# Graph convolutions of a four-layer GNN kernel: two scaled fp16 parts in place of three bf16 parts

## What is computed

```python
def _gcn_conv(x, src, dst, W, b):
    n = x.shape[0]
    h = x @ W
    deg = segment_sum(ones_like(dst), dst, num_segments=n) + 1.0
    dinv = lax.rsqrt(deg)
    norm = dinv[src] * dinv[dst]
    agg = segment_sum(h[src] * norm[:, None], dst, num_segments=n)
    return agg + h * (dinv * dinv)[:, None] + b
...
h = relu(_gcn_conv(x, src, dst, W1, b1))
h = relu(_gcn_conv(h, src, dst, W2, b2))
return _gcn_conv(h, src, dst, W3, b3)
```

## Time and profile before

| | us |
|---|---|
| median of 3 runs | 3300.55 (3297.96 to 3302.93) |
| the profiled execution, its own time | 3305.37 |
| its span | 3303.6 |
| TensorE matmul busy | 2807.4 (85%) |
| VectorE busy | 2368.9 (72%) |
| GpSimd busy | 1212.1 (37%) |
| ScalarE busy | 768.1 (23%) |

### The profile page before, as it was taken

The page is one execution under the profiler, slowest core; times in us unless marked ns, Lnnn a source line. Parts: engine busy times, 40 slices in busy tenths (PEclk is TensorE's granted clock), DMA queues, the critical chain, the costliest instruction groups (busy, mean ns, idle before and its releaser), DMA issues.

```text
span 3303.6 us, 73960 instructions
## 1 busy us (share of the span) xinstructions
PE 2807.4 (85%) x25677; PEld 2263.3 (69%) x25678; DVE 2368.9 (72%) x6272; ACT 768.1 (23%) x1414; POOL 1212.1 (37%) x1205
## 2 busy tenths in 40 slices
PE   3777777899999988998799999999598888988984
PEld 0211121699999987777699999998476777766763
DVE  6988777753333355325798888887699999999986
ACT  0123455520000005001111111111133333332321
POOL 0000000000000000000577777776177777777771
PEclk9999998889999997999899999999599999999896
DMA  0000000000000000000454444443233333433330
GB/s 29 0 0 0 0 0 0 2 2 2 2 2 2 1 1 5 1 1 10 99 132 117 119 115 117 120 119 77 57 104 103 105 105 106 107 104 101 105 97 22
DMA packets 108156, 180.81 MB, mean 55 GB/s; under 512 B 36346, under 2 KB 69900, under 8 KB 107867
## 3 DMA queue, kind: packets, MB, share of 16 engines
q0 software_dynamic: 47824, 89.19, 11.5%
q1 hardware_dynamic: 60043, 87.59, 9.3%
HBM read 171.88 MB, written 4.80 MB: 53 GB/s over the span
## 4 chain that ended last, share of the span: by engine, by line
POOL 32%; issue 10%; DVE 5%; PE 2%; DMA 1%; DVEq 0%; ACT 0%; POOLq 0%; ACTq 0%
POOL gate_rows L1327 20%; POOL msg_rows L956 13%; DVE pre_space L1030 2%; PE msg_sums L1152 1%; PE msg_sums L1167 0%; DMA first_rows<-pre_space 0%; DVE msg_rows L1054 0%; DVE pre_space L1450 0%; DMA msg_rows<-h_rows,all_src_i 0%; PE gate_sums L1581 0%; ACT msg_src_near L968 0%; DMA msg_src_row<-src_rows 0%; DVE pre_space L1122 0%; DVE msg_rows L1050 0%; DVE all_h L1518 0%
## 5 line engine op out<-in xcount | busy, mean ns | idle before, releaser
L1327 POOL DMA_INDIRECT gate_rows<-first_rows,all_src_i x637 | 655.1, 1028 | 198.3 <-issue 193.8
L956 POOL DMA_INDIRECT msg_rows<-h_rows,all_src_i x539 | 535.0, 993 | 164.1 <-issue 163.8
L943 POOL MEMSET pre_middle<- 125x1 f32 x1 | 0.1, 98 | 1590.8 <-POOLq L649 1590.8
L1152 PE MATMUL msg_sums<-pre_parts,pre_space 125*128 125x192 f16 x6125 | 530.7, 248 | 37.5 <-DVE pre_space L1030 37.3
L1152 PEld LDWEIGHTS msg_sums<-pre_parts,pre_space 125*128 125x128 f16 x6125 | 512.3, 99 | 44.3 <-DVE pre_space L1030 39.1
L579 PE MATMUL hop_sums<-dense_work,dense_counts 125*128 125x192 f16 x6250 | 520.7, 247 | 14.0 <-DVE dense_t L533 6.4
L579 PEld LDWEIGHTS hop_sums<-dense_work,dense_counts 125*128 125x128 f16 x6250 | 517.9, 98 | 16.6 <-DVE dense_t L533 6.9
L1556 PE MATMUL gate_sums<-pre_space,pre_parts 125*96 125x384 f16 x2450 | 459.7, 349 | 5.3 <-DVE pre_parts L1424 5.3
L422 PE MATMUL cnt_sums<-cnt_hot,cnt_near 128*128 x1000 | 347.9, 411 | 118.6 <-DVE cnt_hot L361 113.9
L1556 PEld LDWEIGHTS gate_sums<-pre_space,pre_parts 125*96 125x96 f16 x2450 | 315.3, 132 | 140.5 <-issue 30.8
L1030 DVE TENSOR_SCALAR pre_space<-msg_src_near,pre_node_no 125x640 f16<-125x640 f16 x1225 | 393.6, 395 | 11.6 <-ACT msg_src_near L968 11.3
(11 more groups left out here) (261 smaller groups left out, 3320.7 us busy)
## 6 DMA issues: line engine op xcount, KB each, us to landing
msg_edge<-edges SPq DMA_DIRECT2D x98, 384.0 KB
msg_src_row<-src_rows SPq DMA_DIRECT2D x49, 312.5 KB
gate_edge<-edges SPq DMA_DIRECT2D x98, 128.0 KB
gate_rows<-first_rows,all_src_i POOLq DMA_INDIRECT x637
gate_src_row<-on_src SPq DMA_DIRECT2D x49, 187.5 KB
msg_rows<-h_rows,all_src_i POOLq DMA_INDIRECT x539
gate_inputs<-on_edges SPq DMA_DIRECT2D x49, 48.0 KB, 1.9
first_rows<-pre_space SPq DMA_DIRECT2D x6, 375.0 KB
```

The source lines that it names most:

```text
L956: nc.gpsimd.indirect_dma_start(out=rows[:, r, k, :], out_offset=None, in_=table, in_offset=bass.IndirectOffsetOnAxis(ap=src_i[:, at:at + 1 ...
L1152: last = nc.tensor.matmul(got[group % 2][:, n, 0:2 * D], pick[:, c % 2, j, i * EP:(i + 1) * EP], parts[:, j, :], start=(j == 0), stop=(j = ...
L1327: nc.gpsimd.indirect_dma_start(out=rows[:, r, k, :], out_offset=None, in_=table, in_offset=bass.IndirectOffsetOnAxis(ap=src_i[:, at:at + 1 ...
```

## The change

The three bf16 parts become two fp16 parts of a scaled value. fp16 has a narrow range, so the kernel finds in each convolution the largest magnitude of `t` over all nodes, and scales by 30000 over that peak before it rounds.

- In the mixing phase L714 stays. The four splitting steps go; VectorE instead reduces each group to its largest and its smallest value per partition, two full passes over the group.
- After the last group VectorE joins the seven pairs to one value per partition, TensorE transposes that column into one row, VectorE reduces the row to one number, TensorE spreads the number over the partitions by a matmul with a row of ones, and VectorE makes the factor (`peak[:, 3:4]`) and its inverse (`peak[:, 2:3]`).
- Only then ScalarE writes the first parts of all seven groups (scaled by a factor that it reads per partition), and VectorE the second parts, each in one pass.
- The product phase begins with the first group's split. Its matmuls have 192 columns in place of 288; the drain reduces over two parts, and the addition of `t` becomes a multiply-add with the inverse factor.

```diff
-        parts = g["work"][0:NP, 0:NT * 3 * D].bitcast(BF16).rearrange("p (t d) -> p t d", t=NT)
+        parts = g["work"][0:NP, 0:NT * 2 * D].rearrange("p (t d) -> p t d", t=NT)
...
         @block.scalar
-            def split_parts(k, m0, n):
-
-                act.wait_ge(value, k + 1)
-                nc.scalar.activation(parts[:, m0:m0 + n, 0:D], t[:, m0:m0 + n, :], ACT.Copy).then_inc(first, 1)
-                act.wait_ge(rest, k + 1)
-                nc.scalar.activation(parts[:, m0:m0 + n, D:2 * D], h[:, m0:m0 + n, :], ACT.Copy).then_inc(second, 1)
...
-                    if q >= 1:
-                        split_parts(k - 1, *GROUPS[q - 1])
-                split_parts((c + 1) * ngr - 1, *GROUPS[-1])
+                act.wait_ge(scaled, c + 1)
+                for q, (m0, n) in enumerate(GROUPS):
+                    nc.scalar.activation(parts[:, m0:m0 + n, 0:D], t[:, m0:m0 + n, :], ACT.Copy,
+                                         scale=peak[:, 3:4]).then_inc(first, 1)
...
         @block.vector
+            link(nc.vector.memset(ones[:, :], 1.0))
...
                     nc.vector.tensor_tensor(t[:, m0:m0 + n, :], got, spread(dinv[:, m0:m0 + n], D),
                                             ALU.mult).then_inc(value, 1)
-                    dve.wait_ge(first, k + 1)
-                    nc.vector.tensor_tensor(h[:, m0:m0 + n, :], t[:, m0:m0 + n, :], parts[:, m0:m0 + n, 0:D],
-                                            ALU.subtract).then_inc(rest, 1)
-                    dve.wait_ge(second, k + 1)
-                    nc.vector.tensor_tensor(parts[:, m0:m0 + n, 2 * D:3 * D], h[:, m0:m0 + n, :],
-                                            parts[:, m0:m0 + n, D:2 * D], ALU.subtract).then_inc(split, 1)
+                    dve.wait_ge(value, k + 1)
+                    flat = t[:, m0:m0 + n, :].rearrange("p n d -> p (n d)")
+                    link(nc.vector.tensor_reduce(peaks[:, 0, q:q + 1], flat, AX, ALU.max))
+                    link(nc.vector.tensor_reduce(peaks[:, 1, q:q + 1], flat, AX, ALU.min))
+                link(nc.vector.tensor_reduce(peak[:, 0:1], peaks[:, 0, 0:ngr], AX, ALU.max))
+                link(nc.vector.tensor_reduce(peak[:, 1:2], peaks[:, 1, 0:ngr], AX, ALU.min))
+                nc.vector.scalar_tensor_tensor(out=peak[:, 2:3], in0=peak[:, 1:2], scalar=-1.0, in1=peak[:, 0:1],
+                                               op0=ALU.mult, op1=ALU.max).then_inc(peaked, 1)
+                dve.wait_ge(peak_turned, c + 1)
+                nc.vector.tensor_reduce(peak[0:1, 0:1], sums[0:1, 0, 0:NP], AX, ALU.max).then_inc(peaked, 1)
+                dve.wait_ge(peak_spread, c + 1)
+                link(nc.vector.tensor_scalar(peak[:, 2:3], sums[0:NP, 1, 0:1], TINY, 1.0 / TOP, ALU.max, ALU.mult))
+                nc.vector.reciprocal(peak[:, 3:4], peak[:, 2:3]).then_inc(scaled, 1)
+                dve.wait_ge(scaled, c + 1)
+                for q, (m0, n) in enumerate(GROUPS):
+                    dve.wait_ge(first, c * ngr + q + 1)
+                    nc.vector.scalar_tensor_tensor(out=parts[:, m0:m0 + n, D:2 * D], in0=t[:, m0:m0 + n, :],
+                                                   scalar=peak[:, 3:4], in1=parts[:, m0:m0 + n, 0:D], op0=ALU.mult,
+                                                   op1=ALU.subtract).then_inc(split, 1)
...
-                    three = sums[0:NP, 4 * (q % 2):4 * (q % 2) + n, 0:3 * D].rearrange("p n (a d) -> p n d a", a=3)
-                    nc.vector.reduce_sum(v, three, AX).then_inc(drained, 1)
+                    both = sums[0:NP, 4 * (q % 2):4 * (q % 2) + n, 0:2 * D].rearrange("p n (a d) -> p n d a", a=2)
+                    nc.vector.reduce_sum(v, both, AX).then_inc(drained, 1)
                     dve.wait_ge(drained, k + 1)
-                    link(nc.vector.tensor_tensor(v, v, t[:, m0:m0 + n, :], ALU.add))
+                    link(nc.vector.scalar_tensor_tensor(out=v, in0=v, scalar=peak[:, 2:3], in1=t[:, m0:m0 + n, :],
+                                                        op0=ALU.mult, op1=ALU.add))
...
         @block.tensor
                 mix(ngr - 1)
+                pe.wait_ge(peaked, 2 * c + 1)
+                nc.tensor.transpose(sums[0:1, 0, 0:NP], peak[:, 2:3], g["ident"][0:NP, 0:NP]).then_inc(peak_turned, 1)
+                pe.wait_ge(peaked, 2 * c + 2)
+                nc.tensor.matmul(sums[0:NP, 1, 0:1], ones[:, :], peak[0:1, 0:1], start=True, stop=True
+                                 ).then_inc(peak_spread, 1)
...
                     if q == 0:
-                        pe.wait_ge(value, (c + 1) * ngr)
+                        pe.wait_ge(scaled, c + 1)
...
-                            last = nc.tensor.matmul(sums[:, 4 * (q % 2) + i, 0:3 * D], counts[0:NP, at:at + 128],
+                            last = nc.tensor.matmul(sums[:, 4 * (q % 2) + i, 0:2 * D], counts[0:NP, at:at + 128],
                                                     parts[:, j, :], start=(j == 0), stop=(j == NT - 1))
```

More of the change, by code:

```diff
@@ L46 @@
 ROUND = 12582912.0
+TOP = 30000.0
+TINY = 1e-30
 WROW = 28
@@ L656, in convolutions @@
         b_sb = m.sb("b", [NP, 3, D], F32)
+        room = g["work"][0:NP, NT * 2 * D:NT * 3 * D].bitcast(F32)
+        peaks, peak, ones = room[:, 0:16].rearrange("p (i q) -> p i q", i=2), room[:, 16:20], room[0:1, 32:32 + NP]
         sums = m.ps("sums", [128, 8, BANK], F32)
@@ L661, in convolutions @@
         turned = m.sem("turned"); turned_out = m.sem("turned_out"); mixed = m.sem("mixed")
-        value = m.sem("value"); first = m.sem("first"); rest = m.sem("rest"); second = m.sem("second")
+        value = m.sem("value"); first = m.sem("first"); peaked = m.sem("peaked"); scaled = m.sem("scaled")
+        peak_turned = m.sem("peak_turned"); peak_spread = m.sem("peak_spread")
         split = m.sem("split"); summed = m.sem("summed"); drained = m.sem("drained"); passed = m.sem("passed")
```

## The result

The changed kernel takes 3225.74 us (median of four runs, 3217.22 to 3230.84), the kernel before 3299.74 (3297.96 to 3302.93): a ratio of 0.9772, 95% interval 0.9754 to 0.9789, 2.3% faster. Timed again (e1) the ratio is 0.9766 (0.9752 to 0.9780). The profiled execution took 3217.22 us with a span of 3215.5; its counterpart before 3305.37 with 3303.6. The spans differ by 88.1 us, more than the medians (74.0): the profiled execution of the changed kernel was the fastest of its four. That difference is taken apart first.

What follows compares the result with a forecast made beforehand. TensorE's matmuls bound the product phases, chains of handoffs the mixing phases. Terms 73.5 + 1.9 + 1.9 - 0.9 = 76.4 us, from 3300.55 to 3224.2 us, 2.3% faster; range 3215 to 3240.

Steps and rivals of the forecast that it cites:

- Full groups: Product phases: 100 matmuls at 82.5 ns in place of 122.5, each full group 4.0 us less.
- The rival of the weight loads: Product phases: weight loads no longer overlap and set a 98 ns spacing, 29 us less gain, 3253 us; chance 0.04.
- the step that I took from a load's length to the least spacing: Product matmuls: by the skill page, fewer columns stop paying at 106.7 ns, full groups falling only 1.6 us; not adopted.
- First groups: First group of each product phase: first drain 10.5 us after the first product in place of 14.50, 4.0 less.
- The slow stretch: Start of each product phase: half clock again lasts 4.05 us, in which 25 matmuls get done.
- The claim beside it: First group: the first 4 us' clock hardly matters, 0.2 us a convolution; at full clock splits bind, 10.3 us.
- Drain: Drains: reduction 958 ns, multiply-add 558; ends give 0.5 us each; convolution 3 still covered by 0.25 us.
- Mixing phases 2 and 3: Convolutions 2 and 3, first value to first product: 15.0 us in place of 16.89, 1.9 less each.
- Mixing phase 1: Convolution 1: half clock throughout, TensorE sets the pace at 2.45 us a group, products at 1309.7, a 0.9 us loss.
- the signs that the prediction had named: Trace signs, wrong if: spacing above 90 ns, half clock beyond 5 us, factor passes above 600 ns, another message-stage length.
- the costlier search: Search for the peak: dearer crossings cost 4.2 us, slower per-partition-factor passes some 13 us, 3237 us; chance 0.10.
- the half clock through the products: Product phases: TensorE stays at half clock after the new pause, 3363 us if for all 1875 matmuls; chance 0.03.

Runs made afterwards that it cites:

- e1: The changed kernel run again with no edit, for a second trace and a narrower ratio: 3229.99 us, ratio 0.9766.
- e3: Changed kernel with 288 columns again in every product matmul, the third part zero and its sums not read: 3301.4 us, ratio 0.9989.
- e11: Changed kernel with only the first part in products and sums, 96 columns a matmul, leaving out part of the computation: 3177.82 us, ratio 0.9640.
- e7: Changed kernel plus matmuls of no use on TensorE: 4 behind each mix, 30 in the search pause, 16 behind the spreading matmul: 3215.49 us, ratio 0.9754.
- e8: As e7, with the first group's four output tiles innermost in the loop, so each split feeds 16 matmuls, not 4: 3214.97 us, ratio 0.9755.
- e10: Changed kernel with e5's single reduction, e8's loop order, and 14 and 16 matmuls of no use in the two pauses: 3207.34 us, ratio 0.9734.
- e12: The kernel of e5 again, on the same chip as e10: 3210.93 us, ratio 0.9740.
- e5: Changed kernel with one reduction per group to the largest magnitude, in place of one to the largest and one to the smallest value: 3211.59 us, ratio 0.9736.

## Why the prediction was right, step by step

The forecast was 3224.2, the median 3225.74. In the convolutions 76.4 us less was forecast, and 77.0 measured (from the first transpose to the next stage). The terms, with what the first pair of traces shows:

- **Full groups**, 4.0 us each: 12.25 to 8.25 (12.2 to 8.2 right behind a first group) in all fifteen that follow a first group, 60.0 us. Right; e3 shows that the columns alone do it. The rival of the weight loads is refuted by e11. So is the step that I took from a load's length to the least spacing. The Trainium skill, "TensorE: Matmul & The Clock Gate", "LDWEIGHTS (loading the stationary operand)", gives the length alone, 106.7 ns for 128 columns at its columns over 1.2 GHz. The trace shows 98 ns on average in the hops and 102 in e11, for loads that came every 82.5 and every 42.5 ns; so they overlap one another, and their length is no floor under the spacing.
- **First groups**, 4.0 each, 12.0 in sum: 3.90, 4.56 and 3.26, 11.7 in sum. The slow stretch was not always 4.05 us. Busy time by microsecond of the changed kernel, convolutions 1 to 3:

```profile
1313.00:1314.00 1.00, 1.00 (x9) 0.92 (x7) 0.00 (x0) 0.00 (x0) 0.00 (x0) 0.50 0.06 16
1314.00:1315.00 1.00, 1.00 (x13) 0.99 (x12) 0.00 (x0) 0.00 (x0) 0.00 (x0) 0.91 0.00 0
...
1385.00:1386.00 1.00, 1.00 (x9) 0.94 (x8) 0.63 (x2) 0.00 (x0) 0.00 (x0) 0.57 0.00 0
1386.00:1387.00 1.00, 1.00 (x15) 1.00 (x13) 0.00 (x0) 0.00 (x0) 0.00 (x0) 1.00 0.00 0
...
1460.00:1461.00 1.00, 1.00 (x9) 0.96 (x8) 0.00 (x0) 0.00 (x0) 0.00 (x0) 0.52 0.00 0
1461.00:1462.00 1.00, 1.00 (x15) 1.00 (x13) 0.00 (x0) 0.00 (x0) 0.00 (x0) 1.00 0.00 0
```

  The clock rose 4.3 us after the first product in convolution 1, 3.0 in convolution 2, and 5.7 in convolution 3. The prediction's sum, matmuls at 160 ns for that long, the rest of the 100 at 82.5 and 0.27 to the drain, gives 10.6, 10.0 and 11.3 us with these lengths, where 10.60, 9.94 and 11.24 were measured. The working was right; that the three lengths average nearly 4.05 is luck.
- **The claim beside it was wrong**: that the clock of the first 4 us hardly matters, 0.2 us a convolution, since the splits would come one per 0.59 us. Seven of them took 3.49 us, since VectorE does not wait for its own result between them and starts each before the last has ended; at full clock a round is 0.53. With e7 the first drain comes at 9.44 and with e8 at 8.52, so the clock alone is worth 0.5 to 1.8 us a convolution, and clock and feed together 1.4 to 2.7. The first tile, for which I had 3.8 us at full clock, took some 3.0 in e7 (9.44 less 6.19 for the other 75 matmuls and 0.27 to the drain). The sum did not rest on it.
- **Drain**: the reduction 958 ns as taken; the multiply-add 62 ns more than the 558 taken, inside the bounds. The ends give 0.4 us each in place of 0.5. In convolution 3 the cover is 0.05 us and not 0.25. Of the 0.20 between them 0.06 is the multiply-add, and the rest is that I took the whole 3.85 us of idle time before as cover. The short group before shows a round of VectorE with no wait for TensorE:

```profile
1591.04 0.46 DVE L729 TENSOR_REDUCE all_h<-conv_sums 125x96 f32<-125x288 f32 x1
```

  This is 8.55 us after the drain at 1582.49, not 8.40; less 0.40 and plus 0.06 it is the 8.20 measured, within 0.01. Had the factor cost 0.1 us more, VectorE would have set the pace of this convolution.
- **Mixing phases 2 and 3**, 1.9 us less each: 1.6 (16.89 to 15.29). The seventh value comes 10.6 us after the first, as worked out. The transpose with its handoffs was cheaper than taken (0.46 in place of 0.62, from 1379.63 to 1380.09), the spreading matmul dearer (0.66 in place of 0.50), and the two last steps dearer: 0.72 from the start of the first part to that of its remainder (0.57 taken), 0.76 from there to the first product (0.64). No crossing cost the 0.3 more of the upper bound.
- **Mixing phase 1**, a loss of 0.9: a gain of 0.9 (16.04 us against 16.90). The step that failed is that it runs at half clock throughout, so that TensorE with 2.45 us a group sets the pace. Busy time of the changed kernel there:

```profile
1294.00:1296.00 2.00, 2.00 (x12) 2.00 (x11) 1.46 (x3) 0.58 (x1) 0.00 (x0) 0.50 0.00 0
1296.00:1298.00 2.00, 2.00 (x15) 1.98 (x14) 1.66 (x3) 0.58 (x1) 0.00 (x0) 0.72 0.00 0
1298.00:1302.00 4.00, 3.62 (x33) 3.34 (x31) 3.73 (x7) 1.44 (x3) 0.00 (x0) 1.00 0.00 0
```

  The clock rose in the middle of it. In e1's it did too (16.0 us). In e3's trace, with the same mixing phase, it did not, and the phase took 18.18 us (17.8 were forecast for that case). So it goes either way, worth some 2 us; what decides was not shown.

Sum of what the traces show: 60.0 + 11.7 + 1.3 + 3.2 + 0.9 = 77.1 us, the 77.0 of the stage within rounding. That this is so close to the 76.4 forecast is in part luck: convolution 1's mixing phase gave 1.8 us more than forecast, and the other terms together 1.1 less. Luck too is that the median came within 1.5 us of the forecast, since the four runs of the changed kernel spread over 13.6.

Some of the signs that the prediction had named came out against it, each by little. The granted clock stayed at 0.50 for 5.7 us of convolution 3's products (over 5 was to mean wrong), the VectorE passes with the per-partition factor took 0.61 to 0.62 us (over 0.60 was), and the stage from the edge layers on was 12.9 us shorter. Convolution 1's mixing phase took 16.0 us and not 17.8. Of the rivals, the costlier search came true in part (0.3 us in convolutions 2 and 3), and the half clock through the products did not occur in any trace. The forecast did not allow for one thing: it took the edge layers as unchanged, and so they are on average, but they scatter by 14 us, more than every term but the first. That is why the spans of one pair of traces (88.1) would have misjudged the change.

## What to carry to other kernels

Take the spacing of a matmul stream from the distance of its consumers, at the same operand shapes, not from durations or a formula: here one pair of rows gave four fifths of the answer to 1%. A cheaper operand may be bought with a serial step that has no cover (here 6.65 us in convolutions 2 and 3); count it whole, and then ask what part of it need not be there, as the second reduction. Compare traces stage by stage, since an untouched stage can scatter by more than the term in question.

## What was unexpected of the hardware

- 128-column fp16 weight loads, shown at 102 ns each on average, hid behind matmuls spaced 42.5 ns apart (e11).
- Matmuls of no use in the two pauses, 30 in each convolution, were followed by a granted clock at its full level (2.4 GHz) through the start of the products in all three convolutions of e10; the same pauses without them (e12) were followed by half clock (0.50, 1.2 GHz) for the first 2.9 to 3.8 us of products.
- TensorE shown busy for 5.00 of 5.00 us twice over with fp32 transposes and matmuls was granted 1.2 GHz for those 10 us and the five behind them in e5; in the changed kernel, with the same work on TensorE, the clock rose in the middle. The runs do not show what decides.
- VectorE's second parts, which do not wait for one another and take 0.61 us each by their rows, came every 0.53 us; dependent instructions of 0.56 us, with a wait, every 0.59.
